# An expert's weights read at a register's address by TensorE, instead of copied per tile by VectorE

## The reference

```python
def _L0_ffn_ref(x, Wr, br, We1, be1, We2, be2):       # x: (4, 1024, 128), 4 experts, 512 hidden
    logits = jnp.einsum('blh,he->ble', x, Wr) + br
    mask = jax.nn.one_hot(jnp.argmax(logits, axis=-1), NUM_EXPERTS, dtype=x.dtype)
    for e in range(NUM_EXPERTS):
        h1 = jax.nn.relu(jnp.einsum('blh,hf->blf', x, We1[e]) + be1[e])
        oe = jnp.einsum('blf,fh->blh', h1, We2[e]) + be2[e]
        out = out + mask[..., e:e + 1] * oe

x = x + 0.5 * _L0_ffn_ref(_layernorm(x), ...)         # the block of the change, n = 0
x = x + _L0_attn_ref(_layernorm(x), ...)              # causal attention, 16 heads
x = x + 0.5 * _L0_ffn_ref(_layernorm(x), ...)         # the block of the change, n = 1
x = x + 0.5 * _L1_ffn_ref(_layernorm(x), ...)         # 8 experts, 2 chosen
x = x + _L1_attn_ref(_layernorm(x), ...)              # two attention maps
x = x + 0.5 * _L1_ffn_ref(_layernorm(x), ...)
```

## Time and profile before

| what | value |
|---|---|
| median of 3 runs | 3239.93 us (3236.76 to 3244.71) |
| the profiled execution's own time | 3235.5 us |
| its span in the trace | 3233.8 us |
| granted TensorE clock, mean over the span | 0.929 |
| first call of `experts`, first transpose to last output | 124.2 to 229.7 us |
| second call | 899.0 to 999.7 us |

### The profile page before, as it was taken

How to read it: one execution, slowest core, us unless ns; L and a number is a source line. 1 busy time by engine, 2 the same in 40 slices (tenths; PEclk the granted TensorE clock), 3 DMA queues, 4 the chain that set the end, 5 groups by cost and what they waited for, 6 DMA issues and landing times. The chain is left out here.

```text
span 3233.8 us, 61215 instructions
## 1 busy us (share of the span) xinstructions
PE 2509.6 (78%) x18663; PEld 1043.7 (32%) x18790; DVE 2597.0 (80%) x4291; ACT 2238.7 (69%) x2389; POOL 1999.9 (62%) x1358
## 2 busy tenths in 40 slices
PE   1464899998365897488888888888888888883799
PEld 1452333333354454222222222222222222222455
DVE  4446888886555666699999999999999999997665
ACT  2242477777143453289999999999999999992454
POOL 3430122222433454099999999999999999993454
PEclk9986799999586899689999999999999999996799
DMA  3113110110011000200000000000000000000000
GB/s 107 40 53 98 31 30 27 29 29 12 31 43 44 1 1 0 89 12 16 11 12 14 11 13 13 11 15 11 11 15 11 13 14 11 14 1 1 4 11 13
DMA packets 76210, 74.71 MB, mean 23 GB/s; under 512 B 15984, under 2 KB 56440, under 8 KB 75968
## 3 DMA queue, kind: packets, MB, share of 16 engines
q1 hardware_dynamic: 71552, 63.94, 6.8%
q0 software_dynamic: 4544, 9.35, 0.9%
HBM read 48.04 MB, written 24.42 MB: 22 GB/s over the span
## 5 line engine op out<-in xcount | busy, mean ns | idle before, releaser
L1746 POOL TENSOR_TENSOR a_sg<-a_sg,a_shifted 128x1664 f32<-128x1664 f32 x256 | 955.6, 3733 | 21.4
L1943 DVE TENSOR_REDUCE a_mx<-a_pm 128x1 f32<-128x1024 f32 x512 | 619.8, 1210 | 21.6 <-PE a_pm L1785 21.6
L1952 DVE TENSOR_SCALAR a_sg<-a_pa 128x1024 int32<-128x1024 int32 x512 | 619.9, 1211 | 3.6 <-PE a_pa L1785 3.3
L1865 ACT ACTIVATE a_pt<-a_pb 128x1024 f32<-128x1024 f32 x512 | 524.0, 1023 | 107.9 <-PE a_pb L1785 107.9
L1802 PE MATMUL a_po<-a_pt,a_Vh 128*32 128x512 f32 x2048 | 539.1, 605 | 2.2 <-ACT a_sg L1884 2.2
L1802 PE MATMUL a_po<-a_sg,a_Vh 128*32 128x512 f32 x2048 | 539.1, 605 | 0.0
L1743 POOL TENSOR_SCALAR a_shifted<-a_sg,a_parh 128x1664 f32<-128x1664 f32 x256 | 469.5, 1834 | 102.6 <-DVE a_sg L1952 63.9
L1880 ACT ACTIVATE a_sg<-a_sg,a_parh 128x2048 f32<-128x2048 f32 x256 | 511.9, 2000 | 0.0
L1884 ACT ACTIVATE a_sg<-a_sg 128x2048 f32<-128x2048 f32 x256 | 489.8, 1913 | 0.0
L1785 PE MATMUL a_pm<-all_K,all_Q 96*128 96x512 bf16 x1024 | 316.2, 391 | 150.7 <-DVE a_mx L1943 124.6
L1564 ACT ACTIVATE a_pt<-a_ring 128x1024 f32<-128x1024 f32 (+2 forms) x384 | 313.7, 846 | 167.6 <-PE a_ring L1491 164.3
(11 more groups left out here) (278 smaller groups left out, 4763.7 us busy)
## 6 DMA issues: line engine op xcount, KB each, us to landing
all_Q<-q_parts SPq DMA_DIRECT2D x256, 48.0 KB
all_K<-k_parts SPq DMA_DIRECT2D x256, 48.0 KB
k_parts<-p_parts SPq DMA_DIRECT2D x16, 384.0 KB, 2.5
all_Q<-a_rows SPq DMA_DIRECT2D x384, 2.0 KB
e_recs<-routed_rows SPq DMA_DIRECT2D x70, 64.5 KB, 1.9
n_xn<-expert_rows SPq DMA_DIRECT2D x8, 512.0 KB, 6.6
q_parts<-p_parts SPq DMA_DIRECT2D x16, 192.0 KB, 2.3
q_parts<-p_parts SPq DMA_DIRECT2D x8, 384.0 KB, 2.5
```

The source lines that it names most:

```text
L1746: nc.gpsimd.tensor_tensor(buf[:, :, 0:CUT], buf[:, :, 0:CUT], shifted[:], ALU.mult)\
L1865: nc.scalar.activation(pt[(j - LT) % 4][:, i, :], pb[:], ACT.Exp, scale=SC)\
L1943: nc.vector.tensor_reduce(mx[:, (j // PER) % 2, t:t + 1], pm[:], AX.X, ALU.max)\
L1952: nc.vector.tensor_scalar(sg[(j - LS) % 4][:, i, :].bitcast(I32), pa[:].bitcast(I32), SIGN_OFF, None, ALU.bitwise_and).then_inc(abs_done, 1)
```

## The change

`slot` and its copy disappear, with the semaphore `slot_in`. TensorE itself reads `tab[1]` into a register (`weights_of`, right after `turn`) and keeps it for the tile; `hidden` and `output` address `f0w` at that register plus a constant. A tile has 12 different such addresses in `hidden` (three for each of four blocks; the high part is used by two products) and 9 in `output` (two for each of four blocks and the bias), in 16 and 13 products.

```diff
-        slot = m.sb("slot", [P, S, FW], F16)
...
+                at = {}
+
+                def weights_of(j):
+                    at[j] = pe.value_load(tab[0:1, 1, j:j + 1], min_val=0, max_val=(E0 - 1) * FW)
+
                 def hidden(j):
-                    pe.wait_ge(slot_in, j + 1)
                     pe.wait_ge(xh_done, j + 1)
                     pe.wait_ge(xl_done, j + 1)
                     if j >= 2:
                         pe.wait_ge(high_done, j - 1)
                         pe.wait_ge(hid_done, j - 1)
                     for q in range(FT0):
-                        high, low, bias = (slot[:, j % S, lo + q * P:lo + (q + 1) * P] for lo in (0, F0, 4 * F0))
+                        high, low, bias = (f0w[:, bass.ds(at[j] + (lo + q * P), P)] for lo in (0, F0, 4 * F0))
                         out = psh[:, j % 2, q * P:(q + 1) * P]
                         nc.tensor.matmul(out, high, xh[:, j % 3, :], start=True, stop=False)
...
                         high, low = (part[:, j % 3, q * P:(q + 1) * P] for part in (hidh, hidl))
-                        wh, wl = (slot[:, j % S, lo + q * P:lo + (q + 1) * P] for lo in (2 * F0, 3 * F0))
+                        wh, wl = (f0w[:, bass.ds(at[j] + (lo + q * P), P)] for lo in (2 * F0, 3 * F0))
...
-                    nc.tensor.matmul(out, pick[:], slot[:, j % S, 5 * F0:FW], start=False, stop=True)\
+                    nc.tensor.matmul(out, pick[:], f0w[:, bass.ds(at[j] + 5 * F0, P)], start=False, stop=True)\
                         .then_inc(y_done, 1)
 
                 for s in steps:
                     if inside(s):
                         turn(s)
+                        weights_of(s)
...
             def _(dve):
 
-                def weights(j):
-                    at = dve.value_load(tab[0:1, 1, j:j + 1], min_val=0, max_val=(E0 - 1) * FW)
-                    if j >= S:
-                        dve.wait_ge(y_done, j - S + 1)
-                    nc.vector.tensor_copy(slot[:, j % S, :], f0w[:, bass.ds(at, FW)]).then_inc(slot_in, 1)
-
...
-                weights(0)
                 for s in steps:
                     if inside(s):
                         low_x(s)
-                    if inside(s + 1):
-                        weights(s + 1)
                     if inside(s - 1):
                         low(s - 1)
```

More of the change, by code:

```diff
@@ L592, in experts @@
         loaded = [m.sem(f"loaded{r}") for r in range(R)]
-        turned, xh_done, xl_done, slot_in, h_done, hid_done, high_done, low_done, y_done, y_out = (
-            m.sem(x) for x in ("turned", "xh", "xl", "slotin", "h", "hid", "high", "low", "y", "yout"))
+        turned, xh_done, xl_done, h_done, hid_done, high_done, low_done, y_done, y_out = (
+            m.sem(x) for x in ("turned", "xh", "xl", "h", "hid", "high", "low", "y", "yout"))
         steps = range(SLOTS0 + 3)
```

## The result

The changed kernel takes 3301.0 us at the median of four runs (3297.9 to 3304.9) against 3238.4 for the kernel before: 1.0196 times as long, with a 95% interval of 1.0183 to 1.0209. That is 63 us more where 35 were forecast. The profiled execution took 3300.9 us, 65.4 more than that of before.

The account below looks back on a forecast made before the run. The prediction took the ring of six row buffers as the bound, replaced by TensorE's queue: 2.31 + 0.6 + 0.44 = 3.35 us a tile, +35 us with the clock, so 3270.5 profiled and 3275 at the median; range 3234 to 3320.

Parts of the forecast that it names:

- The ring: Six row buffers in experts, from load to landed scatter, set the pace before: 2.7 us a tile, measured 2.8 to 2.9.
- The copy's removal: Dropping the DVE's weight copy in experts shortens a step by 0.1 us at most, 7 us over 70 tiles; forecast 0.
- The address operations: On TensorE's queue, 21 register operations a tile at 0.11 us each, 2.31 us; upper bound 2.7 us.
- The register load and the waits: On TensorE's queue each tile, 0.6 us for the register load and 0.44 us for four wait instructions.
- Head, tail and clock: 1.5 us added to each call of experts for first and last tiles, and +3 us for the lower clock level.
- A: Rival: register operations on TensorE's queue hide in the array's shadow; 3225 to 3240 us, chance 0.16.
- B: Rival: TensorE's products at a register's address are slow themselves; 3495 us, or 3400 at 62 ns a product; chance 0.06.
- C: Rival: the register load stops TensorE's queue longer, 0.3 to 0.7 us more a tile; 3310 us, chance 0.10.
- The signs: Trace marks in experts: 21 register operations and 3.3 to 3.5 us a tile, SP waiting for TensorE, DVE 30 us less busy.
- The bursts of three: Tiles in experts came in bursts of three before; a steady pace from transpose to transpose was to replace them.

Follow-up runs that it names:

- e3: The kernel before with ten row buffers in place of six; 3172.5 us, 0.9799 of the kernel before.
- e1: The changed kernel with all weights at expert 0's constant address, so no register work and no copy; 3224.7 us, 0.9961 of the kernel before.
- e4: The changed kernel with expert 0's constant address (no register work, no copy) and ten row buffers; 3160.5 us, 0.9761 of the kernel before.
- e2: The changed kernel with ten row buffers in place of six, nothing else; 3297.7 us, 1.0185 of the kernel before.
- e9: The changed kernel with a second register load for each tile, used by output; 3346.7 us, 1.0359 of the kernel before.
- e6: The changed kernel with ten row buffers and register addresses in hidden alone, output at constant addresses; 3232.5 us in one run, 2.72 us a tile.
- e7: The changed kernel with ten row buffers, register load kept, one product at its address, other weights at a constant address; 3166.3 us in one run.
- e8: The changed kernel with ten row buffers and the register loaded once, for the first tile, and used for all; 3168.0 us in one run.

## Why the prediction was right, and where its size was off

The direction, the mechanism and the place were right, and 3301 lies in the range of 3234 to 3320. The forecast of 3275 was 26 us short.

*The bound of before.* The ring, as read from the earlier trace rows: shown by e3, which only makes it longer.

*The copy's removal.* Put at 0 to 7 us "and only while the ring is what limits". e1's calls give 6.8, its medians 12. The condition was the wrong way round: where the ring doesn't limit (e3 against e4) the copy costs more, 13 us or 0.19 a tile for the 0.1 at most. I forecast 0 because the queue takes the ring's place, and e2 shows that it does, so neither touched the forecast.

*The address operations.* The count of 21 a tile was exact. The size was the term that failed: "I take 0.11 us: 21 x 0.11 = 2.31". Measured is 0.131 and 2.76 us, above that step's upper bound of 2.7. The 0.45 us between them are 31 us over 70 tiles, more than the whole miss. Two things made it so. The regular distance is 0.124 and not 0.11, some 21 us in all. I took all but the first operation for an ALU_OP of 32 ns, as in the earlier trace rows; all 21 were the fused form of 46 ns. The trace of before, read to the nanosecond, had the difference: in the second expert network an ALU_OP of 32 ns is followed by the next after 0.112 us at the median (three cases), a fused operation after 0.129 (six). And some distances are longer, up to 0.28, which makes the mean 0.131 in both calls, some 10 us more. What stretches them is open; no experiment was aimed at it. With rows of one decimal a distance of 0.11 or 0.13 can't be told apart. It was in the range and not in the forecast.

*The register load and the waits.* 0.6 and 0.44 against 0.65 and 0.44: right, another 3.5 us. e9 shows the load's share by doubling it.

*Head, tail and clock.* A call was to be 35 paces and 1.5 us; 35 x 3.85 = 134.8 is what it takes, with the short first steps making up for the tail, so the 1.5 was not needed. The +3 us for the lower clock level did not come either: the mean clock rose to 1.00 and 0.98, where a lower one was allowed for. Put together, 3270.5 + 31.5 + 3.5 - 3 - 3 = 3299.5 us, for 3300.9 measured in the profiled execution.

*Rivals.* A, operations in the shadow: e2, e6 and e9 refute it where the queue is the bound; every operation there costs its full distance, 9 fewer taking 3.85 to 2.72. But e7 shows a case in which A holds: a queue sum of some 1.2 us under the array's 1.735. The Trainium skill ("Advanced Engine Details and Errata", section Sequencer Loop) has it that other engine instructions can be read and queued while a control instruction executes. e7's trace agrees, with a load of 0.65 us and no longer pace. The sentence doesn't say that control instructions overlap with each other, and in the changed kernel they follow one another at 0.124 us. B, slow products at a register's address: refuted by e8, where all 29 are at such an address, loaded weights and streamed ones alike, at 1.735 us a tile as with constant ones (e4). The 62 ns a product that the Trainium skill gives for one not decoded in hardware ("TensorE: Matmul & The Clock Gate", section "Wait — 56ns, not 53.3ns?") don't appear: in e8 the products start 0.055 to 0.056 us apart. C, a longer register load: 0.65 us instead of 0.6, so no.

*The signs.* The bursts of three are gone, TensorE doesn't wait for rows after the first, and the DVE is some 26 us less busy a call, for 30 foretold. The steady 3.85 us lies above the 3.3 to 3.5 foretold, as the size of the operations has it. Two signs were wrong. From a transpose to the next product of `hidden` it is 0.97 us (180.14 to 181.11), and over 0.6 was to mean C. It doesn't: 0.64 is the load, and the sign had left out the two waits and the first address operation behind it. And SP's waits are still for scatters and not for TensorE (84.8 us in the first call), since a slower output makes its scatter late too. A waiter at the end of a slow ring names its neighbour, not the cause. e2, with four more buffers and the same time, told the two apart.

## What to carry to other kernels

An address from a register costs nothing at the product and one queue instruction for each different address, here 0.13 us where a product takes 0.055: before giving an engine register addresses, count different addresses, register loads and wait instructions for an iteration, and hold their sum against what bounds it now. The 60 us of work in the copy were worth 7 to 12 us behind the ring and 13 without it, since an engine's work costs only where somebody waits for it; a wait that comes round with a fixed number of buffers (line 613) is worth trying first, and four buffers more took off 64 us here. If registers are wanted nonetheless, addresses computed once and reused cost nothing in e8; a kernel that still chooses its expert by tile and does this was not run.

## What the runs showed of the hardware

- TensorE's queue spends 0.124 us from one fused register operation to the next with products between them, though the operation lasts 0.046. A register load from SBUF takes 0.30 us, and 0.65 with its arithmetic and distances. Two wait instructions are 0.106 apart.
- The mean granted clock did not go by the pace: with 30 products a tile in bursts and pauses, at 2.9 us a tile, it was 0.90; with the same 30 at a steady 3.85 us it was 1.00; and at 4.5 us (e9), with longer gaps for the two loads, 0.73 and 0.69. So a slower kernel had the higher clock, until it was slower still. What in the spacing decides is not shown; no run varied it alone.
